# A four-layer residual network on one Trainium2 core: tile 0's gates and soma products moved among the last tile's second linear layer

## The reference

```python
x = x + L0(x)   # gelu(x fc1 + b), then fc2; the last 128 outputs by an expert picked per batch row
x = x + L1(x)   # a linear layer picked per batch row
x = x + L2(x)   # below
x = x + L3(x)   # a linear layer picked per batch row

# L2
ctx = causal_ema(x, tau_ctx)                       # h = alpha*h + x along the tokens
wg = sigmoid(concat([x, ctx]) @ Wg.T + bg);  gated = x * wg
h1 = gelu(x @ Wn1.T + bn1);  mod = 0.5 + sigmoid(h1 @ Wn2.T + bn2)
traces_d = causal_ema(gated * mod[d], tau_d)       # four of them
temporal = sum_d traces_d * softmax(blend)[d]
gate = sigmoid(temporal @ Wtemp.T + btemp);  soma = gelu(x @ Wsoma.T + bsoma)
out = layernorm((soma * gate) @ Wout.T)
```

## Time and profile before

| | us |
|---|---|
| median of 3 runs | 1289.39 (1289.15 to 1289.94) |
| the profiled execution, its own time | 1290.09 |
| its span, first to last instruction | 1288.2 |
| PE busy in it | 1273.0 (99%) |
| DVE busy | 1065.2 (83%) |
| ACT busy | 720.4 (56%) |

### The profile page before, as it was taken

The page is one execution under the profiler, slowest core; times in us unless marked ns, Lnnn a source line. Parts: engine busy times, 40 slices in busy tenths (PEclk is TensorE's granted clock), DMA queues, the critical chain, the costliest instruction groups (busy, mean ns, idle before and its releaser), DMA issues.

```text
span 1288.2 us, 17504 instructions
## 1 busy us (share of the span) xinstructions
PE 1273.0 (99%) x6109; PEld 1067.1 (83%) x6109; DVE 1065.2 (83%) x1682; ACT 720.4 (56%) x1369; POOL 78.9 (6%) x118
## 2 busy tenths in 40 slices
PE   8999999999999999999999999999999999999998
PEld 7788888888888888888887888778888888888877
DVE  7977777787786987777875699999999989998974
ACT  6577565776565875566864343543635353535344
POOL 0010000000000000000000111002100200020000
PEclk9999999999999999999999999989999999999999
DMA  8357554658744658645558898866456555654301
GB/s 291 102 170 236 185 179 131 221 164 266 217 167 151 230 179 264 208 148 171 198 187 273 303 327 327 329 254 220 173 220 238 211 182 208 249 201 160 131 17 66
DMA packets 114288, 262.63 MB, mean 204 GB/s; under 512 B 10345, under 2 KB 32873, under 8 KB 109081
## 3 DMA queue, kind: packets, MB, share of 16 engines
q1 hardware_dynamic: 94336, 183.27, 41.5%
q10 hardware_dynamic: 15032, 62.45, 13.9%
q0 software_dynamic: 4832, 15.79, 3.2%
HBM read 181.19 MB, written 80.28 MB: 203 GB/s over the span
## 4 chain that ended last, share of the span: by engine, by line
PE 86%; DVE 8%; DMA 3%; ACT 1%; issue 1%; ACTq 0%; DVEq 0%
PE bank L1593 29%; PE bank L1595 28%; PE bank L1594 28%; DVE drive L2304 2%; DMA x_slot<-x2hl_dram 1%; DVE drive L2293 1%; DVE temporal L2315 1%; DVE t_lo L2059 0%; DMA x_raw<-in_x 0%; DMA hb_in<-hb_dram 0%; DVE spikes_lo L2059 0%; DVE x_raw L2211 0%; DVE w_hl L2059 0%; DMA mod_t<-mod_dram 0%; PE bank L1901 0%
## 5 line engine op out<-in xcount | busy, mean ns | idle before, releaser
L1593 PE MATMUL bank<-h_hl,w_hl 128*128 128x512 f32 x512 | 199.5, 390 | 0.1
L1594 PE MATMUL bank<-h_hl,w_hl 128*128 128x512 f32 x512 | 199.3, 389 | 0.0
L1595 PE MATMUL bank<-h_hl,w_hl 128*128 128x512 f32 x512 | 199.2, 389 | 0.0
L1593 PE MATMUL bank<-t_hi,sp_hl 128*128 128x512 f32 x448 | 175.2, 391 | 4.4 <-DVE t_lo L2059 1.9
L1594 PE MATMUL bank<-t_lo,sp_hl 128*128 128x512 f32 x448 | 174.4, 389 | 0.0
L1595 PE MATMUL bank<-t_hi,sp_hl 128*128 128x512 f32 x448 | 174.4, 389 | 0.0
L1593 PEld LDWEIGHTS bank<-h_hl,w_hl 128*128 128x128 f32 x512 | 96.1, 188 | 20.8 <-issue 1.1
L1595 PEld LDWEIGHTS bank<-h_hl,w_hl 128*128 128x128 f32 x512 | 96.1, 188 | 20.0
L1594 PEld LDWEIGHTS bank<-h_hl,w_hl 128*128 128x128 f32 x512 | 96.1, 188 | 19.9
L1593 PEld LDWEIGHTS bank<-t_hi,sp_hl 128*128 128x128 f32 x448 | 84.1, 188 | 25.0 <-issue 1.8
L1595 PEld LDWEIGHTS bank<-t_hi,sp_hl 128*128 128x128 f32 x448 | 84.1, 188 | 17.6
(11 more groups left out here) (228 smaller groups left out, 3037.0 us busy)
## 6 DMA issues: line engine op xcount, KB each, us to landing
...
fc_raw<-in_fc_w SPq DMA_DIRECT2D x32, 512.0 KB, 4.2
...
x2hl_dram<-x_hl POOLq DMA_DIRECT2D x28, 512.0 KB, 5.7
x_slot<-x2hl_dram SPq DMA_DIRECT2D x26, 512.0 KB, 5.1
...
```

The source lines that it names most:

```text
L1593: eng.matmul(ps, w_hi, x_hi, start=first, stop=False, skip_group_check=resumed)
L1594: eng.matmul(ps, w_hi, x_lo, start=False, stop=False, skip_group_check=resumed)
L1595: return eng.matmul(ps, w_lo, x_hi, start=False, stop=final, skip_group_check=resumed)
```

## The change

Arithmetic and number of operations stay. What moves:

- TensorE: `n1(0)` goes in front of the last use of tile 6, `mo(0)` behind it; `gate(0, m)` behind uses 2, 4, 6 and 8 of tile 7 (before 4, 7, 9 and 11); `so(0, m)` behind uses 10 to 13 (before: after use 15). Then `n1(1)` and `gate(1, 0)` come before `l1(LAST, 0)` and 1, all four `te(0, m)` follow, and `gate(1, 1)`, `l1(LAST, 2)` and 3 come behind them.
- Banks: `n1(0)`/`mo(0)` in 3, `so(0, m)` in 4, 5, 7, 4, `te`/`ou` of tile 0 in 2, 3, 0, 1, `l1(LAST, m)` in 0, 1, 6, 7; the waits follow the banks. With that `ou(0, 1)`, `(0, 2)`, `(0, 3)` wait for `s_q` of 8, 6 and 7.
- VectorE and ScalarE: the contexts of tile 6 and their copies are done within the passage; those of tile 7 go behind the spikes of tile 0 and, on ScalarE, all four ahead of `wg_tanh(1, 2)` and `q_of(1, 3)`.
- SP: `load_wg(0)` and the contexts of tile 0 are issued earlier, and the rest in a new order; `store_x2(LAST)` goes behind `load_wg(7)` and the four `load_wout`. GpSimd issues the four stores of tile 6's parts together.

The core of the diff (indentation cut by 8):

```diff
-    return bank[m] if t == LAST else bank[KC + m % 2] if t == LAST - 1 else acc_of_tile(t)[m]
+    return bank[(0, 1, 6, 7)[m]] if t == LAST else bank[KC + m % 2] if t == LAST - 1 else acc_of_tile(t)[m]
...
 def n1_bank(i):
-    return bank[5 if i > 1 else 7]
+    return bank[5 if i > 1 else 7 if i else 3]
 def mo_bank(i):
-    return bank[5 if i > 1 else 7]
+    return bank[5 if i > 1 else 7 if i else 3]
 def wg_bank(i, m):
     return bank[((4, 5, 6, 7) if i else (7, 6, 7, 6))[m]]
-def te_bank(m):
-    return bank[m]
-def so_bank(m):
-    return bank[(4, 5, 2, 3)[m]]
+def te_bank(i, m):
+    return bank[m if i else (m + 2) % KC]
+def so_bank(i, m):
+    return bank[((4, 5, 2, 3) if i else (4, 5, 7, 4))[m]]
 def l3_bank(i, m):
...
                 load_raw(K8 * p + k + 3)
             pass_staged(p, k)
+        if p == PAIRS - 1:
+            load_wg(0)
+            for c in range(KC):
+                load_ctx(0, c)
         store_hb(p, K8 - 1, 0)
         if 0 < p < PAIRS - 1:
...
         on.wait_ge(s_fc2, HC * LAST + n)
+    load_xt(0, 0)
+    load_xt(0, 1)
     uses_done(1)
-    load_wg(0)
     pass_staged(PAIRS - 1, K8 + 2)
     uses_done(2)
-    for c in range(KC):
-        load_ctx(0, c)
+    store_ctx(LAST - 2, 1)
+    load_wg(1)
     uses_done(3)
-    load_xt(0, 0)
-    load_xt(0, 1)
-    store_ctx(LAST - 2, 1)
+    load_wg(2)
+    load_wsoma(0)
     uses_done(4)
-    load_wg(1)
+    store_x2(LAST - 1)
     uses_done(5)
-    load_wsoma(0)
+    load_wg(3)
+    load_wsoma(1)
     uses_done(6)
-    load_wg(2)
+    load_wsoma(2)
     uses_done(7)
+    load_wsoma(3)
     load_x(LAST, 0)
     uses_done(8)
-    store_x2(LAST - 1)
+    load_x(LAST, 1)
     uses_done(9)
-    load_wg(3)
-    uses_done(10)
-    load_x(LAST, 1)
-    uses_done(11)
-    load_wsoma(1)
-    uses_done(12)
-    load_wsoma(2)
-    load_wsoma(3)
-    uses_done(13)
     load_wg(4)
+    for c in range(KC):
+        load_ctx(1, c)
+    load_wg(5)
     store_ctx(LAST - 1, 0)
     store_ctx(LAST - 1, 1)
     for c in range(KC):
+        load_slot(1, c)
+    for c in range(KC):
         load_wtemp(c)
-    load_slot(1, 0)
-    load_slot(1, 1)
     load_xt(1, 0)
     load_xt(1, 1)
-    load_slot(1, 2)
-    load_slot(1, 3)
+    load_wg(6)
+    load_wg(7)
     for c in range(KC):
-        load_ctx(1, c)
-    load_wg(5)
-    load_wg(6)
+        load_wout(c)
     store_x2(LAST)
-    load_wout(0)
-    load_wout(1)
...
             eng.tensor_copy(trace_last[:, TAUS * c + d:TAUS * c + d + 1], traced[:, TOK - 1:TOK]
                             ).then_inc(s_tracel, 1)
-    def store_last_hl(c):
-        on.wait_ge(s_fc2, HC * LAST + (9, 11, 12, 13)[c])
-        store_hl(LAST - 1, c)
     for b in range(B):
         on.wait_ge(s_prod, prod_no(0, 4 + b, "P1") + 1)
         load_biases(b)
             store_hl(HALVES * p - 1, c)
     modulation_out(0)
     modulation_back(0)
-    last_columns(0, 0, range(2))
-    store_last_hl(0)
-    last_columns(0, 0, range(2, TAUS))
-    last_columns(0, 1, range(2))
-    store_last_hl(1)
-    last_columns(0, 1, range(2, 3))
-    store_last_hl(2)
-    last_columns(0, 1, range(3, TAUS))
-    store_last_hl(3)
-    for c in range(HALVES, KC):
+    last_columns(0, 0)
+    for c in range(KC):
+        store_hl(LAST - 1, c)
+    for c in range(1, KC):
         last_columns(0, c)
     on.wait_ge(s_made, len(MADE))
     eng.memset(wn2_hl[:, :, :].bitcast(F32), 0.0).then_inc(s_wn2, 1)
...
             on.wait_ge(s_pe["OU"], KC * i)
         else:
-            on.wait_ge(s_fc2, UNITS)
-        eng.activation(even_odd(soma[:, m, :]), halves(so_bank(m)[:, :]), ACT.Gelu, bias=bsoma_sb[:, m:m + 1]
+            on.wait_ge(s_w2lo, UNITS - HC + K8 + m + 1)
...
-            if j == 4:
-                h1_of(0)
+            if j in (5, 7, 9, 11):
+                q_of(0, (j - 5) // 2)
...
-                mod_of(0)
-            if j in (7, 10, 12):
-                q_of(0, (7, 10, 12).index(j))
+                wg_tanh(0, 0)
...
-                wg_tanh(0, 0)
-            if j == 11:
+                for c in range(KC):
+                    x2_hi(t, c)
...
-            if j == 14:
+            if j == 10:
...
-                q_of(0, 3)
+            if j == 12:
...
-            if j == 15:
+            if j == 13:
+                wg_tanh(0, 3)
...
-
-    wg_tanh(0, 3)
+            if j >= 13:
+                soma_of(0, j - 13)
+
...
+    soma_of(0, 3)
     for c in range(KC):
         x1_hi(LAST, c)
-    for m in range(KC):
-        soma_of(0, m)
-    for m in range(SH):
-        temporal_hi(0, m)
     h1_of(1)
     mod_of(1)
     modulation_out(1)
+    for m in range(SH):
+        temporal_hi(0, m)
+    q_of(1, 0)
+    modulation_back(1)
     temporal_hi(0, 3)
-    modulation_back(1)
-    q_of(1, 0)
     wg_tanh(1, 0)
+    for m in range(KC):
+        te_tanh(0, m)
+    for m in range(KC):
+        spikes_hi(0, m)
+    q_of(1, 1)
+    wg_tanh(1, 1)
     for c in range(KC):
         x2_hi(LAST, c)
-    for m in range(HALVES):
-        te_tanh(0, m)
-    q_of(1, 1)
-    te_tanh(0, 2)
-    wg_tanh(1, 1)
-    te_tanh(0, 3)
-    for m in range(SH):
-        spikes_hi(0, m)
     q_of(1, 2)
-    spikes_hi(0, 3)
     ctx_hi(LAST, 0)
     ctx_hi(LAST, 1)
+    ctx_hi(LAST, 2)
+    ctx_hi(LAST, 3)
     wg_tanh(1, 2)
     q_of(1, 3)
-    ctx_hi(LAST, 2)
-    ctx_hi(LAST, 3)
     wg_tanh(1, 3)
     for m in range(KC):
...
         for m in range(KC):
             if at == 0 and t % HALVES == 0 and t:
                 on.wait_ge(s_x2, KC * (t - 1) + m + 1)
+            if at == 0 and t == LAST and m == KC - 1:
+                on.wait_ge(s_mod, 1)
...
-            if m >= 2:
-                on.wait_ge(s_soma, m + 1)
+            if m == 2:
+                on.wait_ge(s_q, KC + 1)
+                on.wait_ge(s_gated, KC)
+            elif m == 3:
+                on.wait_ge(s_mod, 2)
...
     def n1(i):
         if i > 1:
             on.wait_ge(s_soma, KC * (i - 1) + 2)
+        elif i:
+            on.wait_ge(s_soma, 3)
         else:
-            on.wait_ge(s_x1, KC * LAST)
-            if i:
-                on.wait_ge(s_gated, 3)
+            on.wait_ge(s_hlo, use_of_c21(PAIRS - 1, K8 - 1) + 1)
...
             if m == 3:
                 on.wait_ge(s_q, 2)
         elif m:
-            on.wait_ge(s_spk, KC * (i - 1) + (1, 2, 4)[m - 1])
+            on.wait_ge(s_spk, KC * (i - 1) + ((1, 2, 4) if i > 1 else (3, 4, 2))[m - 1])
         else:
...
     def te(i, m):
         if i == 0:
-            on.wait_ge(s_x2, KC * LAST + m + 1)
+            if m < 2:
+                on.wait_ge(s_x1, KC * NT)
+            else:
+                on.wait_ge(s_x2, KC * LAST + m - 1)
         elif m == 0 and i < LAST:
...
     def ou(i, m):
         on.wait_ge(s_spk, KC * i + m + 1)
-        if i < LAST and m != 2:
+        if i == 0 and m:
+            on.wait_ge(s_q, KC + (4, 2, 3)[m - 1])
+        elif 0 < i < LAST and m != 2:
             on.wait_ge(s_q, KC * (i + 1) + (2, 3, 3, 4)[m])
...
         if i == 0:
-            on.wait_ge(s_x2, KC * (LAST - 1) + 3 + m)
-            on.wait_ge(s_q, 3 if m else 4)
+            on.wait_ge(s_x2, KC * LAST)
+            if m < 2:
+                on.wait_ge(s_q, 3 if m else 4)
+            elif m == 2:
+                on.wait_ge(s_gated, 3)
+            else:
+                on.wait_ge(s_soma, 1)
         elif m:
             on.wait_ge(s_gated, KC * i + 2)
         elif i >= 2:
         on.wait_ge(s_wsoma, 16 * KC)
         for c in range(KC):
             mm = so_part(i, m, c)
...
+            if i == 0 and m == KC - 1 and c < 2:
+                mm.then_inc(s_x2free, 1)
...
-        if i == 0:
-            on.wait_ge(s_x1, KC * NT)
-        elif i < LAST:
+        if i < LAST:
...
+            if p == PAIRS - 1 and v == HC - 1:
+                n1(0)
...
             continue
+        mo(0)
         for j in range(HC):
             fc2(2 * HC * p + HC + j)
-            if j == 2:
-                n1(0)
-            if j == 3:
-                mo(0)
-            if j in (2, 3, 4, 5):
-                l1(LAST - 1, j - 2)
-            if j in (4, 7, 9, 11):
-                gate(0, (4, 7, 9, 11).index(j))
-    so(0, 0)
-    so(0, 1)
-    so_pair(0)
+            if j in (2, 4, 6, 8):
+                gate(0, j // 2 - 1)
+            if j in (2, 3):
+                l1(LAST - 1, 2 * j - 4)
+                l1(LAST - 1, 2 * j - 3)
+            if 10 <= j < 10 + KC:
+                so(0, j - 10)
+    n1(1)
+    gate(1, 0)
     l1(LAST, 0)
     l1(LAST, 1)
-    n1(1)
+    for m in range(KC):
+        te(0, m)
+    gate(1, 1)
     l1(LAST, 2)
-    mo(1)
-    gate(1, 0)
     l1(LAST, 3)
     for r in range(1, NT):
         if r > 1:
             n1(r)
             gate(r, 0)
-        for m in range(KC):
-            if r == 1 and m == HALVES:
-                gate(r, 1)
-            te(r - 1, m)
         if r > 1:
+            for m in range(KC):
+                te(r - 1, m)
             gate(r, 1)
...
+            if j == 6:
```

(115 more changed lines are left out.)

46 lines of the change are left out of this document (23 added, 23 removed).

## The result

The changed kernel takes 1298.73 us (median of 4 runs, 1296.76 to 1300.05), the kernel before 1289.66 (1289.15 to 1290.10): a ratio of 1.0070 (95% interval 1.0058 to 1.0082). It is slower by 9.1 us where +3.0 was forecast (1292.4), and lies above the forecast range, which ended at 1296.0. The profiled execution took 1300.05 us, span 1298.3.

A forecast was written before the change was run, and what follows sets the result against it. The prediction took TensorE, busy 99%, as the bound, with VectorE close behind. Moved products 0, the x2 store's path +2.3, with tile 2's late slot +3.0 in all: 1289.4 + 3.0 = 1292.4 us, range 1287.0 to 1296.0.

The forecast's parts named there:

- parts 1 and 2: Tile 0's moved products and the order behind: moved products cost 0; VectorE gains 5 us, then loses it standing still.
- Part 3: Last tile's contexts wait for store_x2(LAST), landing taken at 820.0: VectorE stands still 3.6 us, te(1,0) comes +2.3.
- The wait for `q_sb`: TensorE at the second output product: a new wait of about 7 us for ScalarE.
- Part 4: SP's queue behind the last tile's contexts: n1(2) waits 1.8 to 3.3 us for its slot, te(1,0) at 859.1 to 860.6.
- 4 MB, 10 us: SP's loads of xt(2), the third layer's weights and tile 2's contexts: slot 2 lands near 852.5 to 854.
- the first new wait: TensorE's wait of about 7 us at the second output product, with 2.5 us for the low clock after it.
- the mark: The start of te(1,0) on TensorE, 856.96 before; its shift was taken as the shift of the end, +3.0.
- Rival C: Tile 2's slots land 4 us late and the low clock holds longer: +4.5 to +7, 1295; chance 0.17.
- D: VectorE keeps its 5 us through the te products: faster, 1284.4; chance 0.16 with its lesser forms.
- B: The x2 store isn't held up, landing below 816.4: not slower, te(1,0) 1.2 us sooner, 1288.2; chance 0.15.

The follow-up runs named there:

- e1: The changed kernel with store_x2(LAST) ahead of the four load_wout on SP's queue: 1298.73 us (ratio 1.0079).
- e2: The changed kernel with wg_tanh(1,2) and q_of(1,3) ahead of the four ctx_hi(LAST) on ScalarE: 1299.94 us (ratio 1.0088).
- e6: The kernel of e1 with the two weight loads that ScalarE issues near 822 cut to a twelfth: 1291.19 us (ratio 1.0010).
- e7: The kernel of e5 with the third layer's weights loaded ahead of tile 2's slots, as in the changed kernel: 1295.39 us (ratio 1.0046).
- e3: The changed kernel with the third layer's weights loaded behind tile 2's last slots: 1294.56 us (ratio 1.0046).
- e4: The changed kernel with the edits of e1 and e3 together: 1291.71 us (ratio 1.0015).
- e9: The kernel of e5 with VectorE's order mended, the last tile's contexts ahead of first_sum(1,0): 1288.07 us (ratio 0.9990).
- e12: The kernel of e9 with the four load_wout behind load_wg(7) on SP's queue: 1289.07 us (ratio 0.9999).
- e5: The changed kernel with all l1(LAST) ahead of te(0), other orders fitted to it, and e3's edit: 1295.79 us (ratio 1.0045).
- e8: The kernel before with the third layer's weights loaded behind tile 2's last slots: 1289.29 us (ratio 0.9997).

## Why the prediction was wrong

**Right, and to a few tenths: parts 1 and 2.** No product ahead of `n1(1)` cost anything; `traces_d(0,3)` ended at 783.98 (forecast 784.1), `te(0,0)` began at 788.07 (787.9), `spikes(0,3)` at 799.85 (799.7). VectorE gave back its 5 us by standing still, and was ready for the contexts at 816.7 (816.4). The largest piece of that standing still, 3.19 us, was not foreseen in its place: it came ahead of the first drive of tile 1, in front of the instruction that reads `mod_t`, whose first load had been issued at 785.0 and took 8.0 us to land; but it lies in a time in which I had VectorE idle anyway.

**Part 3: right in mechanism, just past the far end in size.** The store landed at 821.8, forecast 818.6 to 821.6 with 820.0 taken; VectorE stood 5.1 us instead of 3.6. The wait for `q_sb` began and ended about 2 us late, 6.5 us against 7. `ou(0,0)` had waited 1.8 us for the last `wout`, which I had computed (819.0 at worst; it was 819.3) and then not used, although `ou` needs it. `sum_squares(0)` started at 841.25 instead of 839.3.

**Part 4: the step that failed.** It is the term "4 MB, 10 us", from the landing of the context stores, by way of the third layer's weights and the contexts, to the slot at 852.5 to 854: 13 to 14.5 us in all. From the issue of `xt(2)` to the landing of the slot it took 16.3 us (840.73 to 857.07), 2.6 more than the middle of that. Another 1.2 us come from part 3: the context stores landed at 840.7 and not at 839.5. Together they are the 3.8 us by which the slot was later than the middle of its forecast, 853.25.

The trace of before had such a chain: `xt(2)` issued at 833.49, and the slot (line of its chain that ended last: start, us to the landing)

```profile
843.15 6.67 DMA x_slot<-x2hl_dram
```

which makes 849.82, the same 16.3. I priced the chain by bytes over the best rate that a window showed, where a measured one stood in the trace. That the two are equal is luck in part: both slots could be issued only when TensorE had freed the buffer, 9.7 us into the chain before and 7.1 after, and took 6.7 and 9.2 us to land. The other runs say what the weights ahead of the slot cost: with them there the chain took 15.4 to 16.4 us in six kernels (before, after, e1, e2, e6, e7); with them behind it 10.5 to 11.0 in six (e3, e4, e9 to e12), and 14.9 and 13.7 in e5 and e8, where the buffer came free late. So the 2 MB cost about what their bytes say (5.4 us from the changed kernel to e3), and what the term lacked is the rest: 2.5 MB took 10.5 us or more, where 400 GB/s would make it 6.6.

**A clock not counted.** The rest, 2.7 us, is the low clock behind the wait at `n1(2)`. I had it behind the first new wait and not behind the second. From the slot's landing to the mark I took 6.6 us; it was 9.27. Both stretches:

```profile
828.90:834.60 5.70, 5.70 (x14) 4.44 (x15) 5.59 (x11) 0.91 (x2) 0.00 (x0) 0.50 1.00 412
857.07:862.84 5.77, 5.77 (x20) 4.70 (x20) 5.37 (x8) 1.24 (x2) 0.00 (x0) 0.55 0.31 122
```

A wait of 3.8 us was followed by 5.8 us at a granted clock of 0.55, close to the lower level (1.2 GHz). "TensorE: Matmul & The Clock Gate" of the Trainium skill ("HAM oscillation") has gaps throttle the array; these two agree. In e2 the wait at the same place was 1.7 us, and the clock stayed full behind it:

```profile
857.59:863.40 5.81, 5.81 (x34) 4.25 (x35) 5.74 (x8) 1.43 (x3) 0.00 (x0) 1.00 0.29 114
```

There the way from the slot's landing to the mark took 7.1 us.

3.8 and 2.7 make the 6.5 us between the mark that this path forecast (859.1 to 860.6, middle 859.85) and the measured one. Rival C was the right one in kind ("the slots of tile 2 land 4 us late and the low clock holds longer"), at 0.17 and with its price, +4.5 to +7, still 2 to 5 us short of the 9.1. D and B fell: the store was held up, and the 5 us were not kept.

**What lay under it.** I followed each transfer to whoever waits for it, and never asked what the queues as a whole would have to do. The order that I worked out says that nothing can be issued between `load_wg(6)` and `load_wg(7)`; the stretch of 9.5 us at 0 GB/s follows from it without any run. e6 shows that volume makes the landings late, and e12 that an emptied stretch of 4.5 us does so, by 5.3 us at the context store and 1.0 us at the mark and in the median. How many of the changed kernel's 9.1 us are the stretch's stays open: e9, which fills it, changes the orders as well, and e3, e4 and e6 took 4 to 8 us off with the stretch still empty, by taking volume or order out of the slot's way.
